# Expert stages in two groups of unequal size, with one pipeline of pairs, and the first group's routing inside the attention

## The reference

```
x = x + linear_attention(layernorm(x))     # 16 heads of 8, rotary, elu+1 features
x = x + experts(layernorm(x))
x = x + log_attention(layernorm(x))        # causal, 512x512 scores per head, softplus of logs
x = x + experts(layernorm(x))              # the same weights again
```

```
probs = sigmoid(xt @ router_w.T + routing_bias)
topk_p, topk_idx = top_k(probs, 2);  topk_p /= sum(topk_p)
routed = sum over the 2 chosen e of topk_p[e] * (silu(xt @ wg[e].T) * (xt @ wu[e].T)) @ wd[e].T
```

## Time and profile before

| | us |
|---|---|
| median of 3 runs | 1434.26 |
| the profiled execution, its own time | 1436.25 |
| its span, first to last instruction | 1434.5 |
| PE busy | 1031.0 (72%) |
| DVE busy | 693.1 (48%) |
| ACT busy | 642.5 (45%) |
| POOL busy | 454.2 (32%) |
| first attention, from 0 to its last add | 135.9 |
| pairs of `ffn_1`, first to last pair_hidden | 198.2 to 479.8 |
| last add of the log attention | 1087.7 |
| pairs of `ffn_2`, first to last pair_hidden | 1108.8 to 1400.2 |

### The profile page before, as it was taken

The page is one execution under the profiler, slowest core; times in us unless marked ns, Lnnn a source line. Parts: engine busy times, 40 slices in busy tenths (PEclk is TensorE's granted clock), DMA queues, the critical chain, the costliest instruction groups (busy, mean ns, idle before and its releaser), DMA issues.

```text
span 1434.5 us, 21222 instructions
## 1 busy us (share of the span) xinstructions
PE 1031.0 (72%) x7312; PEld 607.1 (42%) x7312; DVE 693.1 (48%) x1482; ACT 642.5 (45%) x938; POOL 454.2 (32%) x529
## 2 busy tenths in 40 slices
PE   4765657875779568788878878777777786776861
PEld 2654535653555323233333333333335564544540
DVE  4885432421333244786777778775544223232311
ACT  1221322523234455777776777775333252432320
POOL 2101333134425143342333323331141404424324
PEclk9996678987899775899998999997768899878876
DMA  9300021122123444353433434311001111212322
GB/s 303 99 0 0 16 65 59 53 63 66 39 83 92 154 143 156 117 165 118 149 119 137 141 112 164 123 45 60 30 23 50 52 58 55 64 43 70 98 58 68
DMA packets 115710, 125.82 MB, mean 88 GB/s; under 512 B 9760, under 2 KB 77984, under 8 KB 115488
## 3 DMA queue, kind: packets, MB, share of 16 engines
q1 hardware_dynamic: 83104, 95.69, 20.4%
q0 software_dynamic: 8192, 16.79, 4.0%
q10 hardware_dynamic: 24320, 12.06, 2.9%
HBM read 62.39 MB, written 62.13 MB: 87 GB/s over the span
## 4 chain that ended last, share of the span: by engine, by line
PE 39%; issue 17%; another core or an unknown queue 13%; DVE 11%; DMA 8%; SPq 6%; ACT 4%; POOL 1%; ACTq 0%; POOLq 0%; DVEq 0%
PE psum L612 11%; DVE ring_b L1611 7%; PE psum L1406 5%; PE psum L639 5%; PE psum L1358 5%; DMA stacks<-stack_qr 3%; PE psum L573 2%; PE psum L623 2%; PE psum L1423 2%; SPq L1754 2%; DMA stacks<-stack_ky 2%; SPq L1749 2%; SPq L1826 2%; PE psum L588 1%
## 5 line engine op out<-in xcount | busy, mean ns | idle before, releaser
L1611 DVE TENSOR_SCALAR ring_b<-psum 128x1024 int32<-128x1024 int32 x160 | 195.7, 1223 | 145.8 <-PE psum L1358 145.7
L612 PE MATMUL psum<-w_expert,ring_a 128*128 x368 | 203.9, 680 | 67.1 <-ACT ring_a L769 60.5
L1485 ACT ACTIVATE ring_a<-psum 128x1024 f32<-128x1024 f32 x160 | 163.2, 1024 | 141.9 <-PE psum L1358 140.4
L1491 ACT ACTIVATE ring_b<-ring_b 128x1024 f32<-128x1024 f32 x160 | 168.3, 1054 | 52.6 <-DVE ring_b L1611 52.6
L1358 PE MATMUL psum<-stacks 32*128 32x128 f32 (+3 forms) x1024 | 105.6, 394 | 116.9 <-DVE ring_b L1611 89.0
L1092 DVE TENSOR_TENSOR ring_b<-psum,ring_b 128x512 f32<-128x512 f32 x96 | 64.2, 669 | 257.5 <-ACT ring_b L754 231.7
L871 POOL DMA_INDIRECT x_sorted<-r_rows,rows_of x128 | 123.7, 966 | 197.3 <-DVE rows_of L1061 161.3
L1715 POOL TENSOR_SCALAR_AFFINE_SELECT ring_b<-ring_b 128x512 f32<-128x512 f32 (+1 forms) x112 | 82.0, 746 | 309.9 <-ACT ring_b L1491 309.9
L878 POOL DMA_INDIRECT r_rows<-y_sorted,rows_of x128 | 122.3, 956 | 115.4 <-DVE x_res L1107 48.7
L1358 PEld LDWEIGHTS psum<-stacks 32*128 32x128 f32 x1024 | 61.9, 197 | 215.0 <-ACT ring_a L1485 83.3
L1603 DVE TENSOR_SCALAR ring_a<-ring_a 128x1024 f32<-128x1024 f32 x160 | 122.9, 772 | 39.5 <-ACT ring_a L1485 39.5
(11 more groups left out here) (168 smaller groups left out, 1326.3 us busy)
## 6 DMA issues: line engine op xcount, KB each, us to landing
ring_a<-x_sorted SPq DMA_DIRECT2D x40, 256.0 KB, 3.4
y_sorted<-y_out ACTq DMA_DIRECT2D x40, 256.0 KB
stack_q<-parts SPq DMA_DIRECT2D x32, 256.0 KB
stack_ky<-parts SPq DMA_DIRECT2D x32, 256.0 KB
stacks<-stack_q SPq DMA_DIRECT2D x32, 256.0 KB
stacks<-stack_ky SPq DMA_DIRECT2D x32, 256.0 KB
stack_k<-parts SPq DMA_DIRECT2D x32, 256.0 KB
stacks<-stack_k SPq DMA_DIRECT2D x32, 256.0 KB
```

The costliest lines, as they stand in the source:

```text
L612: mm = nc.tensor.matmul(bank(2 * (k % 2) + m), x_turned[:, n % 2, (i % 4) * 128:(i % 4 + 1) * 128], w["w_expert"][:, bass.ds(columns[m], 2 ...
L1485: nc.scalar.activation(exps[:, n % RING, 2 * u:2 * u + 2, :], psum[:, first:first + 2, :], ACT.Exp, scale=SCALE).then_inc(self.exp, 1)
L1491: nc.scalar.activation(part, part, ACT.Ln, bias=1.0).then_inc(self.ln, 1)
L1611: nc.vector.tensor_scalar(ring[:, m % RING, HEADS_B[u][0]:HEADS_B[u][1] + 1, :].bitcast(I32), psum[:, first:first + 2, :].bitcast(I32), 0x ...
```

## The change

- `Experts` takes the sizes of its groups: `ffn_1` has groups of 3 and 5 batches, `ffn_2` of 5 and 3. Slots are 31 for 3 batches and 47 for 5, so a stage has 78 slots in 16 + 24 = 40 pairs, and 20 quads.
- The pairs of both groups run in one loop without a drain between them. Orders of PSUM banks are computed in `orders`. `hidden` has 8 buffers in place of 4, the normalised rows of all 8 batches have room, and fetched rows 4 buffers in place of 2 (in the same memory as the normalised rows).
- In `ffn_1` all eight shared batches run between the pairs (after pairs 7, 9, 11, 13, 15). In `ffn_2` three run in the log attention's last steps and five after pairs 1, 3, 5, 7, 9.
- The second group's batches are normalised and turned one per pair from the start of the loop; its scoring is spread over the five pairs after that, then its scattering follows as one sequence: 40 tiles in `ffn_1`, 24 in `ffn_2`.
- The first group of `ffn_1` (3 batches) is normalised, turned and multiplied by the router in steps 2 to 6 of the first attention, scored in steps 6 and 7, and its 24 tiles are scattered from step 7 on. The attention's loop is written out, its projection of v moves ahead of that of k, statistics wait for each batch's own load, and POOL's splitting of the shared weights moves to steps 5 and 6.
- The first group of `ffn_2` has 5 batches and 40 tiles: 3 tiles per step from step k = 12, 18 in all, and the other 22 behind the attention's own POOL work.
- Gathers: in `ffn_1` the first group's 24 tiles after its last quad is stored, and the second group's 40 in steps 1 to 40 of the log attention, one a step, with adds at steps 10, 20, 30, 40, 50. In `ffn_2` the first group's 40 tiles from pair 26 on (the fifth batch behind an add), the second group's 24 at the end.
- The ranks are matmuls in float32r; the constant for them is cast by POOL.

```
+SIZES_1, SIZES_2 = (3, 5), (5, 3)
+            def orders(self):
+                items = [("shared", b, c) for b in self.shared_first for c in range(IC)]
...
+                for j in range(self.all_pairs):
+                    items.append(("pair", j))
...
         def a_tensor_step(pe, b):
+            if 1 <= b - AHEAD - 1 <= ffn_1.sizes[0]:
+                ffn_1.tensor_logits(pe, b - AHEAD - 1)
...
+            if b == 7:
+                ffn_1.tensor_ranks(pe, 0)
...
+            if 1 <= b - AHEAD <= ffn_1.sizes[0]:
+                ffn_1.turn(pe, b - AHEAD)
...
         def a_vector_step(v, b):
+            if b == 6:
+                ffn_1.vector_first(v, 0)
+            if b == 7:
+                ffn_1.vector_gates(v, 0)
+                ffn_1.vector_place(v, 0)
...
         def attn_a_pool(p):
+            ffn_1.send(p, 0)
...
             def lead_pool(self, p, k):
+                if last + 7 <= k < 18:
+                    self.send_tiles(p, 0, 3 * (k - last - 7), 3 * (k - last - 6))
...
             def pool(self, p):
+                if self.led:
+                    self.send_tiles(p, 0, 3 * (11 - self.sizes[0]), 2 * self.tiles(0))
+                for b in range(self.first_late, B + 1):
+                    self.pool_rstd(p, b)
+                self.send(p, 1)
+                for b in range(1, self.first_late):
+                    self.fetch(p, b)
...
             def vector(self, v):
+                for j in range(self.all_pairs):
+                    if late + j <= B:
+                        self.vector_bias(v, late + j)
+                    if j == self.scored + 1:
+                        self.vector_logits(v, 1)
+                    self.pair_hidden(v, j)
+                    for b in self.shared_after.get(j, ()):
+                        self.vector_shared(v, b)
...
+                    if j == self.scored + 4:
+                        self.vector_place(v, 1)
...
+        ffn_1 = Experts("f1", AttentionDone(), SIZES_1, shared_first=(),
+                        shared_after={7: (1,), 9: (2, 3), 11: (4, 5), 13: (6, 7), 15: (8,)}, adds_after={22: (1,), 25: (2,), 27: (3,)})
+        ffn_2 = Experts("f2", log_attn, SIZES_2, shared_first=(1, 2, 3),
+                        shared_after={1: (4,), 3: (5,), 5: (6,), 7: (7,), 9: (8,)}, adds_after={30: (1,), 33: (2,), 35: (3,), 38: (4,)},
+                        led=True)
```

More of the change, by code:

```diff
@@ L412, in attn_a_pool @@
[L412 to L413 removed]
+            for b in range(1, B + 1):
+                if b + 2 <= B:
+                    na.pool_rstd(p, b + 2)
+                if 1 <= b - AHEAD + 1 <= ffn_1.sizes[0]:
+                    ffn_1.pool_rstd(p, b - AHEAD + 1)
+                if b == 4:
+                    p.wait_ge(loaded, 16 * len(rest_loads))
+                    nc.gpsimd.tensor_copy(const["earlier"][:], earlier_room).then_inc(split_low, 1)
+                if b in (5, 6):
+                    g = b - 5
+                    whole, high, low = w["w_expert"][:, g * INNER:(g + 1) * INNER], w_shared[:, g, 0, :], w_shared[:, g, 1, :]
+                    nc.gpsimd.tensor_copy(high, whole).then_inc(split_high, 1)
+                    p.wait_ge(split_high, g + 1)
+                    nc.gpsimd.tensor_tensor(low, whole, high.bitcast(F32), ALU.subtract).then_inc(split_low, 1)
@@ new lines, in turned_x, with pair_slots, quad_slots @@
+            def turned_x(self, b):
+                return x_rows[:, B - 1].rearrange("p t n -> p (t n)") if not self.led and self.is_early(b) else xT[:]
+            def pair_slots(self, j):
+                g = 0 if j < self.pairs[0] else 1
+                j -= g * self.pairs[0]
+                return g, [i for i in (2 * j, 2 * j + 1) if i < self.slots[g]]
+            def quad_slots(self, n):
+                g = 0 if n < self.quads[0] else 1
+                first = 4 * (n - g * self.quads[0])
+                return g, first, min(4, self.slots[g] - first)
@@ new lines, in last_pair_item, with shared_count @@
+            def last_pair_item(self, n):
+                return self.items.index(("pair", 2 * n + 1))
+            def wait_read(self, v, k):
+                if k < 0:
+                    return
+                kind, *which = self.items[k]
+                if kind == "shared":
+                    v.wait_ge(self.shared_y, self.shared_count(which[0]))
+                else:
+                    v.wait_ge(self.h_turned, which[0] + 1)
+            def shared_count(self, b):
+                return 1 + [c for kind, c in self.down_bank if kind == "shared"].index(b)
@@ L1223, in vector @@
                 if not self.following.takes_rest:
-                    self.add_routed(v, B - 1)
-                    self.add_routed(v, B)
+                    for b in range(1, B + 1):
+                        if not any(b in some for some in self.adds_after.values()):
+                            self.add_routed(v, b)
         DUS, LAG = 10, 6
```

1110 lines of the change are left out of this document (534 added, 576 removed).

## The result

The changed kernel takes 1395.21 us (median of 4, 1390.48 to 1399.93), the kernel before 1433.91 beside it: ratio 0.9728, 95% interval 0.9693 to 0.9764. It is faster, by 39 us, but 81 us slower than the 1314 of the prediction and outside its range of 1268 to 1370. Its profiled execution took 1390.48 us, with a span of 1388.7.

What follows compares the result with a forecast made beforehand. No engine was near full; stalls, exposed routing, group changes and late PE updates were taken to cost the time. Terms -38 - 44 + 10 + 22 - 80 + 9 = -121 from 1436.25 gave 1315.2, stated as 1314 us; range 1268 to 1370.

Steps and rivals of the forecast that it cites:

- The charge for late updates: In long POOL tile sequences PE's updates reach ACT late, about one per 5 us; charged 10, 47, 20 and 46 us.
- nothing passes: Rival: in long sequences fewer or no PE updates get through, +54 us at the middle, 1369 us; chance .18.
- the work of the stages without any late update: Whole kernel with every charge for late updates taken off the forecast: 1191 us.
- First attention: Start to first pair: 198.2 becomes 160 us (-38), with 13 us for work added to DVE, bounds 0 to 25.
- Pairs of `ffn_1`: First expert stage's 40 pairs: 282 becomes 238 us (-44), or 191 if lateness costs nothing.
- no gap at the sixteenth pair: Sign of being right: in `ffn_1` the pairs run on at the sixteenth without a gap.
- Log attention and front: Log attention +10 us for more tiles, adds and PE work; stretch before `ffn_2`'s first pair 21 becomes 43 (+22).
- Pairs of `ffn_2`: Second expert stage's pairs: 291.5 becomes 211 us (-80), bounds 164 and 240.
- End: After the last pair: +9 us, as the last gather is 24 tiles instead of 16.
- clean pair: Expert stages: a pair with nothing beside it takes 3.0 to 3.1 us.
- missing drain: Pairs of `ffn_1`: no drain remains at changes of group, so three times 8.6 us go.
- Slower: Rival: tensor engine's clock falls to 1.2 GHz through both pair stages, 1463 us with nothing passing; chance .05.

Runs made afterwards that it cites:

- the measuring kernel: Kernel computing nothing of the reference: PE and a partner pass a token 28 times beside POOL's transfers; 48.4 us a phase undisturbed, 75.5 beside one 40-tile scatter.
- the undisturbed run: The changed kernel, unedited, on a chip where no update is late: 1273.34 us against 1288.17 for the kernel before, ratio 0.9876.
- e1_gap_bias: Changed kernel with four POOL memsets after every tile, plus the expert bias moved behind `vector_hat` in the first attention: 1347.35 us against 1353.04 without the move.
- groups of 4: Kernel before, with POOL waiting after every 4 tiles of a long sequence until they have landed: 1335.7 us, ratio 0.9344.
- e1_after_gap: Changed kernel with four one-column POOL memsets after every tile of a long sequence: 1353.0 us, ratio 0.9454 to the kernel before.

## Why the prediction was wrong

*The charge for late updates was right in its sum by luck, and wrong in its law.* The changed kernel loses 1395 - 1273 = 122 us by them (medians on different chips; 115 between the two profiled executions); the prediction's charges were 10 + 47 + 20 + 46 = 123. By stretch (table, after less none late) they are 6, 41, 10, 58: none is met closely, and the errors cancel. The law behind them, one update per 5 us at a steady rate, was wrong: the delay grows within a sequence (rounds of 3.8, 4.9, 8.4, 11.2 us in the measuring kernel, where 1.8 is normal; waits of 9.2, then 30.2 in the changed kernel's gather). Its readings were off too: the first remote wait of the earlier trace rows ends 12.1 us behind the start of the sequence, not 8, and the two pairs in that stretch take 12.7 and 11.2 us, not 20 together. So the rival "nothing passes" described the long gaps better, yet its +54 did not come: it is not why 1395 was measured.

*The step that failed is the work of the stages without any late update*: predicted 1191, measured 1273. Term by term:

- **First attention: DVE's addition, +13 taken, with bounds 0 to 25.** The steps from 44.09 to 129.91 alone are 22 longer than five of 12.75. I had counted 15 us of added instructions (about 2.5 us a step for each of three batches, then the scoring) and let the waits absorb some. They did the reverse: a 1.12 us wait for the rstd stands at the head of the step, ahead of `vector_hat`, which PE waits for (`e1_gap_bias`: one line moved, 4.8 us less in the attention). What is left, about 2 us, was not traced. Where nothing is late, the first pair is 17 us later than predicted (167.0 against 150): the 24 tiles leave from 125.95 to 155.50 and not from 117 to 147, and the first pair follows 10.6 us behind the end of the last.
- **Pairs of `ffn_1`: 191 predicted, 223.7.** Rows of DVE, POOL and PE of the undisturbed run show the largest part, the 16th pair:

```profile
277.41 0.69 DVE L1204 TENSOR_TENSOR ring_b<-psum,ring_b 128x512 f32<-128x512 f32 x1 [1.66 <-ACT ring_b L863]
297.72 0.42 DVE L1204 TENSOR_TENSOR ring_b<-psum,ring_b 128x256 f32<-128x256 f32 x1 [19.62 <-ACT ring_b L863]
```

```profile
289.47 0.96 POOL L950 DMA_INDIRECT x_sorted<-r_rows,rows_of  x1 [0.30 <-issue]
```

```profile
294.31 1.11 PE L743 MATMUL psum<-identity,ring_a 128*128 128x128 f32 x4 [16.24 <-DMA ring_a<-x_sorted]
```

  The second group's first quad needs the 40th tile, which leaves at 289.47. 40 tiles are 50 us, and only the pairs up to the 15th, with four shared batches among them, stood beside them. The 16th pair still belongs to the first group, whose rows are long there; it waits because PE's list has the turn of the second group's first quad ahead of its gate_up, and the shared batch 8 stands behind both. I had the start of the sequence and its length, counted on "no gap at the sixteenth pair" and gave a wait for the last tile no price: 17 us. (In the profile on a chip with late updates this gap can't be seen, since the pairs are held up until the sequence is over.) Most of the rest is in the pairs that carry adds (27.3 us for six, 8.7 above 3.1 each, where adds and last quads together had 4), in those of the end (3.5 to 3.9, as they lead the log attention), 4, and in the 9th to the 13th pair, which carry shared batches and scoring.
- **Log attention and front: 641 predicted, 664.4.** That is +35 us over before, where +12 was predicted without late updates (+10 for the log attention, +2 for the front). Its steps up to the 65th take as long as before. Then come those with the first group of five batches. All engines and the clock in the same ten steps of the tail (columns: stretch, its length, busy time and count of PE, its loads, DVE, ACT, POOL, granted clock, DMA share, GB/s), before and after:

```profile
975.00:1047.00 72.00, 50.16 (x387) 22.94 (x386) 41.38 (x83) 32.03 (x45) 13.97 (x18) 0.79 0.13 43
```

```profile
935.20:1024.00 88.80, 61.62 (x425) 31.25 (x418) 44.34 (x93) 39.02 (x59) 14.22 (x19) 0.69 0.10 35
```

  16.8 us more, of which DVE's busy time is 3 and ACT's 7; on the undisturbed chip it is 89.0 too. I had taken 3 us for PE and 7 for adds. PE is busy 11.5 us more, for 10% more matmuls, at a lower clock (0.69 against 0.79); how much of it is the clock, and what makes these steps longer, was not measured apart and stays open. The first pair of `ffn_2` then waits for the 40th tile: in the undisturbed run that leaves at 1043.70, and the pair comes at 1055.07.
- **Pairs of `ffn_2`: 164.5 predicted, 175.3.** Pairs beside the adds of the last ten take 5.1 to 7.5 us.
- **End: +9 predicted, +9.2.** Right. The clean pair of 3.0 to 3.5, the missing drain (3.3 us at the change of group in `ffn_2`) and 6.3 for a shared batch (15.6 for a pair with two) were right.

In short: the sum gave nothing to the wait for the last tile of a larger group, too little to steps of the two attentions that take over routing work, and too little to pairs that carry adds.

*What the 39 us are.* Where nothing is late the change is worth 14.8 us (1288.17 - 1273.34). The other 24 are late updates, if the two kinds of chip differ in nothing else: before loses 146 (1433.91 against 1288.17, different chips), the changed kernel 122. A part of this is the tensor engine's clock: the mean granted clock of before is 0.85 with late updates and 0.89 without, and 0.88 with groups of 4 on a late chip. Sixteen pairs less (eight in each stage, 48 us) and six changes of group less (52, both at the prediction's prices) should have brought about 100; by the stretches above they came back as longer attention steps, the log attention's tail and waits for the last tile of larger groups. The kernel before has no profile on an undisturbed chip, so this account is not exact.

*Slower* did not come near: the clock recovers behind each gap, as the slices of 9 behind the 5 and 6 show.

## What to carry to other kernels

Larger groups save fixed costs, and their last transfer comes later: for each group ask what work stands beside its whole sequence, and who waits for its end. Work put into a loop is not priced by its busy time; if it waits at the head of a step, the whole loop behind it becomes longer. Run the kernel before on more than one chip ahead of explaining its gaps: here 146 of 1434 us were there on some chips and not on others, and an edit that gained 59 us on one lost 54 on another. And look in the trace whether a pause is one: four memsets after each tile moved the tiles apart by 0.05 us.

## What the runs showed of the hardware

On three of five chips, an uninterrupted sequence of POOL's indirect DMAs, one per 1.14 to 1.31 us, delays the semaphore updates of PE. In the measuring kernels the first late round begins 12 to 21 us behind the start (30 with a pause after every 16 tiles), a round takes up to 11.2 us where 1.79 is normal, so an update is up to 9.4 us late, and the last late round ends 2 to 11 us behind the end. In the kernel before the first late result was finished 8.7 us behind the start of its sequence (PE at 217.81, the first tile at 209.15); in the changed kernel one was seen 42 us late; in both all is normal 3 to 6 us behind the end. Why it is 42 us there and 9.4 in the measuring kernel is open.

DVE and ACT passing a token without PE are not delayed (33.4 to 33.5 us for 28 rounds, on a chip with late updates and on one without); POOL waits a little for its own memsets (18 waits marked remote, 19.3 us, in `e1_after_gap`). Direct DMAs of SP, POOL's computing, and tiles that are 1.56 us apart do not delay PE. What mechanism it is was not found.

The Trainium skill, "SBUF — State Buffer", section "Who interferes with whom", has PE and ACT never waiting on anyone. The prediction took that as a statement on this delay, and the trace as its refutation. The section speaks of the engines' ports into SBUF, and nothing here contradicts it: PE's four transposes take 1.11 to 1.12 us in the rounds that are late and in those that are not, and what comes late is the news that they are done.
